# A decoder kernel on one core: experts for each batch, or once over sorted tokens

## The reference, cut to what matters

```
logits = z @ Wg + bg                       # (512, 8)
e      = argmax(logits)                    # one expert for each token, the first where two are equal
h      = gelu(z @ W1[e] + b1[e])           # 256 -> 256
x      = x + h @ W2[e] + b2[e]             # 256 -> 256, then the output
```

## Time and profile before

| what | us |
|---|---|
| median of 3 runs | 2138.87 |
| lowest and highest run | 2138.83 and 2142.31 |
| span of the profiled execution | 2139.7 |
| TensorE busy in it | 1961.1 |
| DVE busy | 1713.5 |
| ACT busy | 1318.5 |
| POOL busy | 260.0 |

### The profile page before, as it was taken

One profiled execution on the slowest core, in us unless ns is written; L12 is line 12 of the kernel. 1 busy time (PEld: TensorE's weight loads), 2 busy tenths in 40 slices (PEclk: granted clock), 3 DMA queues, 4 the chain that ended last, 5 costly groups with the idle time before them and its releaser, 6 DMA issues.

```text
span 2139.7 us, 42900 instructions
## 1 busy us (share of the span) xinstructions
PE 1961.1 (92%) x17874; PEld 1108.8 (52%) x17874; DVE 1713.5 (80%) x2676; ACT 1318.5 (62%) x1957; POOL 260.0 (12%) x280
## 2 busy tenths in 40 slices
PE   4999988899999998889999998898999999889898
PEld 2677742424667773232566776333265777533235
DVE  8888878795878877699588887869878888786956
ACT  5666647386366655748546664565944666455682
POOL 1000001350000001035000000103500000011430
PEclk8999999999999999999999999999999999999999
DMA  6366700030055561012006665002001666300200
GB/s 275 75 127 129 142 32 13 10 113 11 21 103 129 126 120 34 6 32 91 11 21 126 126 127 124 12 2 102 22 11 44 133 123 130 94 13 9 94 2 11
DMA packets 424210, 156.39 MB, mean 73 GB/s; under 512 B 405928, under 2 KB 416560, under 8 KB 423120
## 3 DMA queue, kind: packets, MB, share of 16 engines
q1 hardware_dynamic: 423440, 151.54, 30.0%
q0 software_dynamic: 576, 2.10, 0.3%
HBM read 43.43 MB, written 2.16 MB: 21 GB/s over the span
## 4 chain that ended last, share of the span: by engine, by line
PE 62%; DVE 27%; ACT 5%; DMA 3%; issue 3%; POOL 0%; POOLq 0%; DVEq 0%; ACTq 0%; SPq 0%
DVE nmx L2052 14%; PE ps L655 11%; PE ps L657 11%; PE ps L656 11%; PE ps L1033 6%; PE ps L823 4%; PE ps L817 3%; PE ps L818 3%; PE ps L1019 3%; DMA arena<-arena 2%; PE ps L983 1%; DVE st L1691 1%; DVE arena L1862 1%; PE ps L1043 1%; PE ps L1100 1%
## 5 line engine op out<-in xcount | busy, mean ns | idle before, releaser
L2052 DVE TENSOR_REDUCE nmx<-ps 128x2 f32<-128x1024 f32 x384 | 444.7, 1218 | 15.2 <-PE ps L983 13.6
L1557 ACT ACTIVATE arena<-ps 128x512 f32<-128x512 f32 x768 | 406.3, 600 | 50.8 <-PE ps L1019 45.9
L655 PE MATMUL ps<-arena 128*128 128x512 f16 (+1 forms) x784 | 266.6, 340 | 1.3 <-DVE arena L1783 1.1
L657 PE MATMUL ps<-arena 128*128 128x512 f16 (+1 forms) x784 | 266.5, 340 | 0.0
L656 PE MATMUL ps<-arena 128*128 128x512 f16 (+1 forms) x784 | 266.5, 340 | 0.0
L1849 DVE TENSOR_SCALAR_CACHE_REDUCE ps<-ps 128x1536 f32<-128x1536 f32 x128 | 225.7, 1763 | 40.5 <-PE ps L657 39.8
L1033 PE MATMUL ps<-arena 128*17 128x256 f32 x3072 | 240.4, 389 | 0.0
L1862 DVE SCALAR_TENSOR_TENSOR arena<-arena,rs 128x1536 f16<-128x1536 f32 x128 | 231.6, 1810 | 4.2 <-ACT arena L1447 4.2
L1447 ACT ACTIVATE arena<-arena,rs 128x1536 f16<-128x1536 f32 x128 | 200.8, 1569 | 42.9 <-DVE rs L1855 42.9
L1440 ACT ACTIVATE arena<-ps,nm 128x1536 f32<-128x1536 f32 x128 | 197.1, 1540 | 10.3 <-DVE ps L1849 10.3
L817 PE MATMUL ps<-arena 128*128 128x128 f16 x1536 | 185.3, 219 | 1.6 <-DMA arena<-arena 1.6
(11 more groups left out here) (286 smaller groups left out, 3732.9 us busy)
## 6 DMA issues: line engine op xcount, KB each, us to landing
arena<-in_experts SPq DMA_DIRECT2D x4, 3840.0 KB, 11.5
arena<-in_weights SPq DMA_DIRECT2D x8, 929.0 KB, 19.1
arena<-arena SPq DMA_DIRECT2D x72, 64.0 KB, 2.1
arena<-in_ctx SPq DMA_DIRECT2D x4, 1024.0 KB, 5.3
arena<-arena SPq DMA_TRANSPOSE x256, 3.2
arena<-in_ctx_t SPq DMA_DIRECT2D x4, 1024.0 KB, 4.9
arena<-arena SPq DMA_DIRECT2D x72, 32.0 KB, 1.9
y<-in_x POOLq DMA_DIRECT2D x4, 512.0 KB, 4.2
```

The costliest lines, as they stand in the source:

```text
L655: mm(out_, lh, rh, start=(k == 0), stop=False)
L657: last = mm(out_, ll, rh, start=False, stop=(k == n - 1))
L1557: A(pr_[:, n % RING, :], ps[:, 4 + n % 3, :], ACT.Exp).then_inc(b_exp.sem, 1)
L2052: V.tensor_reduce(nmx[:, g_ % 2, ch, :, pp, i], ps[:, 2 * (z % 2):2 * (z % 2) + 2, :], AX.X, ALU.max, negate=True)\
```

## The change

The expert stage of each batch is taken out. In its place:

- **In each batch**, `next_window(b + 1)` does what lay between the experts: context and row transposes, query and key products of the next window stage. Statistics and rows of the next batch are computed in cross attention (`next_stats`, `next_moments`, `next_rows` in `attend`), into a buffer `xn` that SP loads there. The normalised rows `zf` are split (`rows_hi` on ACT, `rows_lo` on DVE) into a buffer `zx`, of which a row holds the split row, the row of `x` (copied by SP, `keep_rows`) and the token's number: 520 words of 4 bytes. SP transposes the split rows by four DMA transposes (`transpose_rows`), from which TensorE makes the logits (`route_logits`) inside the next `windowed`; DVE chooses (`route_choice`), TensorE counts how many tokens before this one chose the same expert (`route_ranks`), and DVE makes a place for each token (`route_slots`). POOL writes the rows there by four indirect transfers (`scatter_rows`) into `zx_d`, a tensor in the chip's main memory with a region for each expert. `scaled_hi` and `scaled_lo` of the next latent stage wait once for them, because `zx` lies in a buffer that they write.
- **Once, in the last batch**, SP loads the expert weights and POOL splits them, and POOL writes pad rows behind each region's rows (`pad_regions`, eight transfers, 5376 rows).
- **At the end**, `experts()`: logits, choice, slots and scatter of the last batch, small tables of which expert owns which block (`block_tables`), and then 23 blocks (`NB`: 16 full ones and up to 7 that are partly padding) of 128 tokens. For each, SP reads its place from the table and loads 128 rows by one plain transfer into a ring of six (`BR`); TensorE transposes the four 128x128 pieces (`turn_block`), ACT copies them out; TensorE reads the block's expert from the table (`value_load`) and makes hidden layer and output with weights at an address that depends on it; ACT applies GELU, DVE splits and adds, and POOL writes the rows to the output by an indirect transfer in which rows of padding are left out (`scatter_block`).

The core of the diff:

```diff
-            def expert_hidden(b, e, par, only=range(DC)):
-                for m in only:
-
-                    last = product(ps[:, 2 * par + m, :],
-                                   [(tuple(ewc[:, bass.ds(2 * e * EW + HE * part + D * c + P * m, P)] for part in range(2)),
-                                     both(zT, slice(None), c)) for c in range(DC)])
+            def next_window(t):
+
+                transpose_context(t)
+                transpose_next(t)
+                pe.wait_ge(lx_added.sem, lx_added.at(t - 1, 2 * NT))
+                window_keys(t, range(4))
+
+            def block_hidden(j):
+
+                at = pe.value_load(where[0:1, 0, j:j + 1], min_val=0, max_val=2 * (NE - 1) * EW)
+                pe.wait_ge(e_zt.sem, e_zt.at(0, j + 1))
+                for m in range(DC):
+                    if j >= 2:
+                        pe.wait_ge(e_gelu.sem, e_gelu.at(0, 2 * (j - 2)) + m + 1)
+                    last = product(ps[:, HID_BANK[j % 2][m], 0:P],
+                                   [(tuple(ewc[:, bass.ds(at + (HE * part + D * c + P * m), P)] for part in range(2)),
+                                     (zb[j % 3][:, c, :], zb[j % 3][:, DC + c, :])) for c in range(DC)])
                     last.then_inc(e_h.sem, 1)
+                return at
...
+            def block_out(j, at):
...
+                mm(d_, chosen, b2h[:], start=True, stop=False)
+                mm(d_, chosen, b2l[:], start=False, stop=False)
+                for c in range(DC):
+                    hi, lo = (hgT[j % 2][part][:, c, :] for part in range(2))
+                    wh_, wl_ = (ewc[:, bass.ds(at + (2 * HE + HE * part + D * c), D)] for part in range(2))
+                    mm(d_, hi, wh_, start=False, stop=False)
+                    mm(d_, hi, wl_, start=False, stop=False)
+                    last = mm(d_, lo, wh_, start=False, stop=(c == DC - 1))
                 last.then_inc(e_y.sem, 1)
 
-            def routed(b):
...
-                for e in range(NE):
-                    if 0 < e < NE - 1:
-                        expert_hidden(b, e + 1, (e + 1) % 2)
...
-                    expert_out(b, e, e % 2)
+            def experts():
+                route_logits(B - 1)
+                route_ranks(B - 1)
+                pe.wait_ge(ew_lo.sem, 2 * NE)
+                pe.wait_ge(e_table.sem, e_table.at(0, 1))
+                at = [None] * NB
+                turn_block(0)
+                turn_block(1)
+                for j in range(NB + 1):
+                    if j < NB:
+                        at[j] = block_hidden(j)
+                    if j + 2 < NB:
+                        turn_block(j + 2)
+                    if j:
+                        block_out(j - 1, at[j - 1])
...
# on SP, at the end
+            transpose_rows(B - 1)
+            sp.wait_ge(zx_out.sem, zx_out.at(B, 16 * NE))
+            sp.wait_ge(e_table.sem, e_table.at(0, 1))
+            for j in range(NB):
+                r_ = j % BR
+                at = sp.value_load(where[0:1, 1, j:j + 1], min_val=0, max_val=NE * REGION - P)
+                if j >= BR:
+                    sp.wait_ge(e_h.sem, e_h.at(0, 2 * (j - BR)) + 2)
+                    sp.wait_ge(o_out[r_].sem, 16 * (j // BR))
+                sp.dma_start(block[r_], zx_d[bass.ds(at, P), :]).then_inc(block_in[r_].sem, 16)
...
# on POOL: after the norms of each batch, and at the end
+            def scatter_rows(b):
+
+                pool.wait_ge(r_slots.sem, r_slots.at(b, 1))
+                pool.wait_ge(z_lo.sem, z_lo.at(b, 1))
+                pool.wait_ge(xc_in.sem, xc_in.at(b, 16))
+                if b == B - 1:
+                    pool.wait_ge(zx_out.sem, zx_out.at(b, 16 * NE))
+                for i in range(NT):
+                    pool.indirect_dma_start(zx_d, bass.IndirectOffsetOnAxis(slot[:, i:i + 1], 0), zx[:, i, :], None)\
+                        .then_inc(zx_out.sem, 16)
...
+            def scatter_block(j):
+
+                r_ = j % BR
+                pool.wait_ge(e_added.sem, e_added.at(0, j + 1))
+                pool.indirect_dma_start(out.rearrange("b s d -> (b s) d"), bass.IndirectOffsetOnAxis(row_at[:, r_:r_ + 1], 0), xb[r_][:, 0:D], None,
+                                        bounds_check=B * S - 1, oob_is_err=False).then_inc(o_out[r_].sem, 16)
```

More of the change, by code:

```diff
@@ L87, in at, with again @@
         return b * self.per_batch + n + self.credit
+    def again(self, before):
+        s_ = Signal.__new__(Signal)
+        s_.sem, s_.per_batch, s_.credit = self.sem, 0, before
+        return s_
 class Order:
@@ L190, in decoder @@
         mask_raw = lay.take([4, 2 * P])
+        span = lay.take([P])
         assert lay.at <= 81920
@@ new lines, in route_ranks @@
+            def route_ranks(b):
+                before, every = prefix[:, 0:P], prefix[:, P:P + 1].to_broadcast([P, P])
+                d_ = ps[:, RANK_BANK, 0:NT * NE]
+                pe.wait_ge(r_onehot.sem, r_onehot.at(b, 1))
+                mm(d_, before, oh16.rearrange("p t e -> p (t e)"), start=True, stop=False)
+                for i in range(NT - 1):
+                    n = NT - 1 - i
+                    mm(d_[:, NE * (i + 1):].rearrange("p (t e) -> p t e", t=n), every,
+                       oh16[:, i:i + 1, :].to_broadcast([P, n, NE]), start=False, stop=(i == NT - 2))
+                for i in range(NT):
+                    last = mm(ps[:, RANK_BANK, NT * NE:NT * NE + NE], every, oh16[:, i, :], start=(i == 0), stop=(i == NT - 1))
+                last.then_inc(r_ranks.sem, 1)
@@ L1319, in _ @@
                 cross_attention(b)
-                routed(b)
-        @block.scalar
+                if b < B - 1:
+                    next_window(b + 1)
+            experts()
+        @blk.scalar
         def _(act):
@@ L1658, in _ @@
                 cross_attention(b)
-                routed(b)
-        @block.vector
+                if b < B - 1:
+                    next_window(b + 1)
+            experts()
+        @blk.vector
         def _(dve):
@@ L2240, in late_constants, with experts @@
+            def experts():
+                normalise(B - 1, 4, x, zf)
+                rows_lo(B - 1)
+                route_choice(B - 1)
+                route_slots(B - 1)
+                block_tables()
+                for j in range(NB + 1):
+                    if j < NB:
+                        split_block(j)
+                    if j:
+                        finish_block(j - 1)
             def late_constants():
```

405 lines of the change are left out of this document (247 added, 158 removed).

## The result

| | before | after |
|---|---|---|
| median of the runs | 2139.45 us (4 runs, 2138.83 to 2142.31) | 2157.51 us (4 runs, 2152.24 to 2160.29) |
| ratio, 95% interval | | 1.0085 (1.0067 to 1.0104) |
| profiled execution, span | 2139.7 us | 2150.5 us |

The change makes the kernel 0.85% slower, a small difference but clear of the noise. The forecast was 2122 us, 0.8% faster; the time lies in its range of 2088 to 2180.

A forecast was written before the change was run, and what follows sets the result against it. TensorE, busy 92% of the span, was taken as the bound. 2139.7 - 108.6 + 14.1 - 50.7 + 24.8 + 98.3 + 4.9 = 2122.5 us, forecast as 2122 us, range 2088 to 2180.

The forecast's parts named there:

- Bound now: Whole kernel: TensorE bounds it, busy 92% of a span of 2139.7 us and never stopping around the experts.
- the boundaries: Between batches, three times: eight experts removed, a chain stays; gain 36.2 us each, -108.6 us together.
- Routing inside the window stage: Next batch's window stage: router and slot operations, DMA transposes and scatters add 4.7 us per boundary, +14.1 us (9 to 28).
- a sign of being wrong: At the boundary: PE waiting for the DMA transposes would show the forecast wrong; 1.0 us was taken for this wait.
- Moved statistics at no price: Last third of cross attention: next rows' statistics cost nothing; uncovered they would cost 3.3 us for each batch.
- Pads "0 (up to 8 us)": Last batch, POOL between context split and cross keys: eight pad transfers (11.2 MB) counted as 0, up to 8 us.
- Front of the last stage: Last batch ahead of the first block: a chain with TensorE nearly still, +24.8 us (19 to 32).
- Period 4.2: Block loop: array 1.8, register instructions 1.3, load 1.0, with waits 4.2 us a block; 23.4 periods, +98.3 us.
- the first, the ring: Block loop: the ring of six is the bound, 8.8 us over 2.5 periods, 3.5 us a block, 2106 us; chance 0.20.
- rival 2: Block loop: register instructions cost 0.2 us each, load 1.4, period 6.0 us, total 2164; chance 0.24.
- rival 3: Block loop: array busy less than half the time, clock near 0.5, period of 6; chance 0.09.
- Tail: Behind the last output product: DVE's addition 0.5, POOL's scatter 1.2 and its landing 3.0 (+0.2), +4.9 us.

The follow-up runs named there:

- e5: e1 with the pads' rows read from SBUF (128 partitions) and not from one row of HBM: 2083.43 us, 0.9726 of before.
- e1: The changed kernel with the five new small tiles declared behind the arena and not ahead of it: 2131.31 us, 0.9956 of before.
- e2: The kernel before with one unused tile of 32 bytes per partition declared ahead of the arena: 2160.17 us, 1.0086 of before.
- e6: e1 with a ring of eight block buffers and not six: 2121.6 us, 0.9913 of before.
- e7: e1 without TensorE's load of the block's weight address and its arithmetic, every block using the first expert's weights: 2127.6 us.
- e14: The kernel before with an unused tile of 256 bytes per partition ahead of the arena: 2139.9 us, one execution.

## Why the prediction was wrong, point by point

- **Bound now** (TensorE, 92%): right. The removed work left the path: 119.9 us at the boundaries for 108.6 forecast. The mask addition of the second batch stands at 537.4, not 533.8, but its batch was already 7.8 us late: from the projection it takes 18.0 us, where the working gave 22.2. The step that was over-sized is the row of matmuls ahead of the scores: 24 of 512 columns (526.67 to 532.0 us), where the working had 42.
- **Routing inside the window stage** (+4.7 each): over-sized. With the arena in place the three batches differ from before by -0.8, +1.1 and (first batch, without routing) -0.5 us, so it is hidden within about 2 us. TensorE waits 2.4 us for the four DMA transposes at the first boundary, which the prediction had named as a sign of being wrong; no such delay is left at the self projection. The scatters take 0.96 us each (median of 16, one 1.93), not 1.2.
- **Moved statistics at no price**: held; self to cross projection is 0.5 us shorter in each batch.
- **Pads "0 (up to 8 us)"**: this is the step that failed. They cost about 55 us, of which 47.9 came back with a faster source (e5). I looked at GpSimd, which had nothing to do, and at how few transfers run there, and not at who waits for each of those few (L553). The term was volume by rate, 11.2 MB, at a rate that no row of before showed; at 127 GB/s it is 88 us of full engines, and each of the four small transfers in it then takes 15 us. The bound from above that such a rate gives was missing.
- **What the prediction did not name at all**: the address. The new tiles cost 26 us through the DMA transposes (e1), 20 in the kernel before (e2). Nothing in the trace of before could show it; the order of declarations in the diff did.
- **Front of the last stage** (+24.8): right. From the finished router rows (first projection addition 2046.5 + 5.5) to the first turn at 2075.9 it is 23.9 us.
- **Period 4.2**: the second wrong size. 14 x 0.09 for register instructions and 1.0 for the load were laid end to end with the array. A block has twelve such instructions of 0.046 us, one of 0.151 and a SEQ_ASSERT of 0.018, together 0.72, and the load takes 0.302, less than the 1.0 of the prediction. Half of this 1.0 us runs beside the matmuls: it adds 0.5 to 0.6 us to a block (e6 against e7) where 2.3 were charged. From the first turn to the last addition (2142.7) it is 67 us and not 98. Of the rivals it was the first, the ring, that came: from a block's addition to the reloaded place it had 8.8 us, and the chain shows 7.3 to 7.9; a block then takes 2.96 us and not 3.5.
- **Rivals 2 and 3** (dear registers, clock): the time of rival 2 (2164) lies near what was measured, but not for its reason: its period was 6.0 and the measured one 2.75, with 0.046 us for most register instructions and not 0.2. A total that is hit this way proves nothing. Nor did the clock of rival 3 come: it was near 0.5 only up to 2080 us, the first 4 us of the loop, and 0.98 to 1.00 behind them. What a clock of 0.5 costs the array stands in the trace of before: matmuls of 256 columns start 0.213 us apart at 0.50 (33 to 36 us) and 0.109 at 1.00 (from 525.5 us on).
- **Tail** (+4.9): 7.7 us from the last addition (2142.8) to the end at 2150.5.

The measured span less the two is 2150.5 - 55 - 26, about 2070 (2083.4 was measured with both mended, the pads still there): with every term that the prediction worked out at its measured size, the forecast would have been too high by 50 us, and its sign right. The sign hung on a term of 0 and on one that was missing. That the time lies in the stated range is luck: 81 us that nobody had counted stand against 50 that were charged too much.

## What to carry to other kernels

Before a bulk transfer is put where "few transfers run", list the small transfers in that stretch and who waits for them, and price it as bytes over the rate of its own pattern; a row that is written a thousand times comes from SBUF (about 375 GB/s here), not from one row of HBM (127). When a diff adds tiles, write down the start address of every buffer that a DMA transpose reads, before and after: declare new ones behind the large buffers (e1, 3.2 us for a transpose), or pad to 256 bytes (e14, 3.2 us). In a ring, count how many blocks pass in a lap in the program's order before adding prices of instructions; and where a ring is the bound, leaving work out does not show what the work costs.

## What the runs showed of the hardware

- A DMA transpose of the latent stage takes 3.2 us where its source starts at a multiple of 256 bytes and 3.7 where it does not (offsets of 32, 64, 128 and 480 bytes alike), worth 20 to 27 us in the 256 of the kernel before (272 in the changed one).
- 5376 rows of 2080 bytes written to HBM: 127 GB/s when all come from one row of HBM, 236 to 306 (one slice 179) from eight rows in fewer packets, about 375 from 128 partitions of SBUF.
- Beside the slow stream at full share the 8 KB transfers of another queue took 15.1 to 15.7 us, and its 32 KB transfers 14.7 in place of 1.9; beside the faster stream the waits were 6.3 us in all.
- A TENSOR_LOAD on TensorE's queue takes 0.302 us, a fused register instruction 0.046 or 0.151; one load, 13 of these and a SEQ_ASSERT of 0.018 add 0.5 to 0.6 us to a block of 24 matmuls; an indirect scatter of 128 rows holds GpSimd for 0.96 us (into `zx_d`) or 0.98 (into the output), medians both, and one into the output lands after 2.1 to 3.8.
- The same block loop at the same ring was granted 0.98 to 1.00 in one kernel (from 2080 us on) and 0.72 to 0.94 in another (from 2060 us on), and took 60.5 and 67.1 us; why the clock came back in one is open.
